# One Trainium2 core, a gated cross-attention layer with eight experts: weight pieces two to a slot, a router in column groups, contexts scored by VectorE

## The reference

```python
def xattn(ctx, adj, W, b):                    # adj is the layer-normed x
    si = einsum('bnd,d->bn', ctx, W[0, :256]); sj = einsum('bnd,d->bn', ctx, W[0, 256:])
    return 0.6 * sigmoid(si[:, :, None] + sj[:, None, :] + b[0]) + 0.4 * adj

def ffn(x, wg, W, b):                         # 4096 tokens of 1024, 8 experts
    logits = x @ wg; probs = softmax(logits); idx = argmax(probs); gate = probs[idx]
    return gate * (x @ W[idx].T + b[idx])     # top-1 routing

x = x + tanh(g_xattn) * xattn(ctx, layernorm(x), ...)
x = x + tanh(g_ffn) * ffn(layernorm(x), ...)
```

## Time and profile before

| what | us |
|---|---|
| median of three timed runs | 689.08 |
| lowest and highest of them | 683.34, 689.30 |
| profiled execution, span | 687.3 |
| TensorE busy | 576.6 (84%) |
| VectorE busy | 445.2 (65%) |
| GpSimd busy | 331.8 (48%) |
| ScalarE busy | 274.1 (40%) |

### The profile page before, as it was taken

How to read it: one execution, slowest core, us unless ns; L and a number is a source line. 1 busy time by engine, 2 the same in 40 slices (tenths; PEclk the granted TensorE clock), 3 DMA queues, 4 the chain that set the end, 5 groups by cost and what they waited for, 6 DMA issues and landing times.

```text
span 687.3 us, 14019 instructions
## 1 busy us (share of the span) xinstructions
PE 576.6 (84%) x2841; PEld 461.2 (67%) x2842; DVE 445.2 (65%) x557; ACT 274.1 (40%) x408; POOL 331.8 (48%) x489
## 2 busy tenths in 40 slices
PE   7898889888707969979779997995999799699990
PEld 5576667666505848858567885884888588588870
DVE  3357778697699885856784587588378557843420
ACT  2367766686424333413333333333343233333220
POOL 1446777788623336325336533633633364356540
PEclk8569999999957989989989998997999899899995
DMA  7911577576679876764776497577756656545530
GB/s 262 403 40 33 175 261 237 198 217 223 239 258 259 238 214 190 225 208 152 224 220 196 147 243 213 189 219 215 217 168 204 189 166 198 164 132 186 182 126 13
DMA packets 83666, 134.72 MB, mean 196 GB/s; under 512 B 11568, under 2 KB 64304, under 8 KB 83504
## 3 DMA queue, kind: packets, MB, share of 16 engines
q1 hardware_dynamic: 73712, 99.47, 49.4%
q0 software_dynamic: 9792, 33.82, 12.8%
HBM read 99.44 MB, written 35.91 MB: 197 GB/s over the span
## 4 chain that ended last, share of the span: by engine, by line
PE 27%; DVE 23%; issue 19%; ACT 9%; POOL 7%; DMA 6%; DVEq 3%; POOLq 2%; ACTq 2%; SPq 1%
PE pair L1058 12%; DVE wt L782 7%; PE pair L985 4%; DVE xr L718 4%; ACT wt L598 4%; DVE pair L777 4%; PE pair L996 3%; PE pair L969 3%; PE pair L974 3%; ACT rb L617 2%; DVE rows L804 2%; DMA out_x<-rows,scatter_row 2%; DMA rows<-table 1%; DVE xc_tr L725 1%; POOL out_x L500 1%
## 5 line engine op out<-in xcount | busy, mean ns | idle before, releaser
L1058 PE MATMUL pair<-wt,xt 128*128 x1728 | 416.2, 404 | 62.6 <-DVE rows L804 41.6
L1058 PEld LDWEIGHTS pair<-wt,xt 128*128 128x128 f32 x1728 | 336.9, 196 | 141.5 <-issue 66.5
L488 POOL TENSOR_TENSOR rows<-rows,rb 128x1024 f32<-128x1024 f32 x37 | 88.7, 2398 | 164.2 <-ACT rb L617 162.6
L782 DVE TENSOR_TENSOR wt<-pair,wt 128x1024 f32 (+1 forms) x64 | 77.5, 1212 | 32.7 <-ACT wt L598 32.7
L598 ACT ACTIVATE wt<-pair 128x1024 f32 (+1 forms) x64 | 64.2, 1024 | 77.7 <-DVE pair L777 70.1
L604 ACT ACTIVATE xt<-pair 128x1024 fp32r<-128x1024 f32 x38 | 39.0, 1026 | 133.0 <-DVE pair L790 110.6
L777 DVE STREAM_TRANSPOSE pair<-w_raw 128x1024 f32<-128x1024 f32 x64 | 79.7, 1250 | 1.9
L790 DVE STREAM_TRANSPOSE pair<-xb 128x1024 f32<-128x1024 f32 x38 | 47.7, 1255 | 46.5 <-issue 26.3
L804 DVE SCALAR_TENSOR_TENSOR rows<-pair,scal,rows 128x1024 f32<-128x1024 f32 x36 | 46.0, 1278 | 44.6 <-PE pair L1058 44.2
L617 ACT ACTIVATE rb<-bias_bc,scal 128x1024 f32 (+1 forms) x37 | 46.0, 1244 | 48.4 <-POOL scal L485 41.1
L794 DVE TENSOR_TENSOR xt<-pair,xt 128x1024 fp32r<-128x1024 f32 x38 | 46.4, 1221 | 28.1 <-ACT xt L604 25.9
(11 more groups left out here) (123 smaller groups left out, 417.9 us busy)
## 6 DMA issues: line engine op xcount, KB each, us to landing
w_raw<-in_L_ffn_W SPq DMA_DIRECT2D x256, 128.0 KB
xb<-table SPq DMA_DIRECT2D x156, 128.0 KB
rows<-table SPq DMA_DIRECT2D x38, 520.0 KB
xr<-in_x SPq DMA_DIRECT2D x32, 512.0 KB, 6.9
ctx_in<-in_ctx SPq DMA_DIRECT2D x8, 512.0 KB, 4.9
bias_bc<-in_L_ffn_b SPq DMA_DIRECT2D x8, 512.0 KB
out_x<-rows,scatter_row POOLq DMA_INDIRECT x36, 4.2
table<-xr,pos POOLq DMA_INDIRECT x32, 4.5
```

The source lines that it names most:

```text
L488: nc.gpsimd.tensor_tensor(rows[:, k, 0:H], rows[:, k, 0:H], rb[:, :], ALU.add).then_inc(base_ready, 1)
L782: nc.vector.tensor_tensor(where[:, :, 1].rearrange("p a k o -> p (a k) o"), ps[:, :].rearrange("p (k o) -> p k o", k=K), where[:, :, 0].re ...
L1058: last = nc.tensor.matmul(out_ps[r % 2][:, HALF * h:HALF * (h + 1)], xt[:, r % RING, x_part, k, :], wt[:, bass.ds(par, 1), w_part, k, HALF ...
```

## The change

- **Weight pieces.** Every expert now gets at least four slots (LEAST = 4), and each of the first four slots of an expert turns two pieces of the next expert's weights (STEP = 2). `w_raw` holds two pieces instead of four; the pair for the next slot is asked for when both pieces of this one are turned, in four transfers of 256 KB. The bias comes in quarters.
- **Slots.** The rows are turned one slot ahead instead of two, `xt` has two buffers instead of three, `rows` four instead of three. The loops have turns of 4 written-out slots (TensorE 2). The first 32 slots (SURE) run without a test; 28 more may be used, so the loops go to 60 instead of 42.
- **Squares.** ACT squares the rows in the slot (`square` on `rows`) and not in the tile stage; POOL waits for it.
- **Router.** The router's weights are padded to 32 columns, and the eight blocks go to four column groups of the array (`tile_position=(0, j)`), two in each; the copy of the logits has 128 rows and a folding matrix `fold` adds the four groups.
- **Transposed tiles.** They have one PSUM buffer (pair 0) instead of two; ACT copies both halves, DVE none.
- **Contexts.** Groups 0 and 1 are scored by DVE straight from the loaded rows (16 instructions of 128x256 with a running sum, two diagonal matrices of 128x512) and spread by one matmul each. Groups 2 to 7 are turned behind tiles 0, 2, 5, 7, 13 and 15.
- **First weights.** The first expert's pieces are turned behind tiles 9, 11, ... 23, and cut behind the next tile. SP asks for them between the loads of x tiles; from the third on, the load waits until the piece two before is turned, and x tiles queue behind it.
- The small loads of the start go through ACT's queue.

```diff
+    LEAST = 4
+    STEP = K // LEAST
+    RING = 4
+    TURN = 4
+    SURE = E * LEAST
+    SLOTS = SURE + N // P - LEAST
+        CTX_TURN = {0: 2, 2: 3, 5: 4, 7: 5, 13: 6, 15: 7}
+        PIECE = {9 + 2 * m: m for m in range(K)}
 @sync
+            def load_first_piece(m):
+                if m >= STEP:
+                    sp.wait_ge(w0_turned, m - STEP + 1)
...
             for t in range(RX, T):
+                if t % 2 and t // 2 - 6 < K:
+                    load_first_piece(t // 2 - 6)
                 sp.wait_ge(row_stored[slot_of(t)], 16)
...
+            def slot(t, r, i):
+                kind = sp.value_load(slot_tab[0:1, 0, bass.ds(t, 1)], min_val=0, max_val=2)
+                rows2, rows3 = row_of(t + 2), row_of(t + 3)
+                if not (isinstance(t, int) and t < 2):
+                    settled(out_stored[(r + 2) % RING], 16 * i + 16 * (r // 2))
+                load_rows(sp, rows2, r + 2)
+                with sp.If(kind > 1):
...
+                    settled(w_turned, STEP * g + STEP)
+                    load_pieces(row0)
+                settled(xb_turned, t + 2)
+                load_blocks(sp, rows3, r + 3)
 @gpsimd
+                settled(sq_ready, u + 1)
+                nc.gpsimd.tensor_scalar(scal[:, k, 0:1], scal[:, k, 8:9], 1.0 / H, EPS, ...)
 @scalar
+            def slot(t, r, i):
+                k = (r + 1) % RING
+                square(t + 1, k, i + (r + 1) // RING)
+                xt_high(t + 1, (r + 1) % 2, cut_a)
+                exp_sum(t + 1, k)
+                with act.If(kind > 1):
+                    for m, ps in enumerate((cut_b, cut_a)):
+                        settled(w_turned, STEP * g + m + 1)
...
+                scaled_bias(t + 1, k, e1, act.snap(e1 % 2))
 @vector
+            def score(t, place_, w0, scale):
+                return nc.vector.scalar_tensor_tensor(out=junk[t], in0=ctx_in[...], scalar=scale,
+                    in1=w_flat[:, w0:w0 + D], op0=ALU.mult, op1=ALU.mult, accum_out=place_)
...
+                if t in PIECE:
+                    first_turn(PIECE[t])
+                if t - 1 in PIECE:
+                    first_low(PIECE[t - 1])
...
+            def slot(t, r, i):
+                settled(xt_ready, t + 1)
+                turn_rows(t + 1, k, TURN // 2 * i + (r + 1) // 2)
+                with dve.If(kind > 1):
...
+                    settled(w_ready, STEP * g + K)
+                    settled(w_landed, 64 * g + 64)
+                    turn_piece(0, cut_b)
+                    xt_low(t + 1, k)
+                    settled(xt_ready, t + 2)
+                    turn_piece(1, cut_a)
+                    cut_low(0, cut_b)
+                    cut_low(1, cut_a)
+                    settled(w_ready, STEP * g + K + STEP)
+                with dve.Else():
+                    xt_low(t + 1, k)
+                settled(base_ready, t + 1)
+                nc.vector.tensor_scalar(scatter_row[...], rows[..., TOK:TOK + 1].bitcast(I32), beyond[:, bass.ds(t, 1)], None, ALU.max)
+                settled(summed, t + 1)
+                nc.vector.scalar_tensor_tensor(...).then_inc(finished, 1)
+            with dve.Fori(0, SURE // TURN) as i:
+                for r in range(TURN):
+                    slot(TURN * i + r, r, i)
+            with dve.Fori(SURE // TURN, SLOTS // TURN) as i:
+                for r in range(TURN):
+                    with dve.If(work > 0):
+                        slot(TURN * i + r, r, i)
 @tensor
+                pe.wait_ge(xc_copied[1], t + 1)
                 for k in range(K):
+                    j = COLS * (k % 4)
+                    last = nc.tensor.matmul(lgt_ps[j:j + COLS, r, :], wg_sb[:, k, :], xc_tr[:, t % 2, k, :],
+                                            start=(k < 4), stop=(k >= K - 4), tile_position=(0, j))
```

More of the change, by code:

```diff
@@ L275, in _ @@
         def _(sp):
-            for g in range(2):
-                sp.dma_start(ctx_in[:, g, :], group_of(ctx_t, g)).then_inc(ctx_landed[g], 16)
-            with nc.allow_non_contiguous_dma(reason="512 weights, once, as columns"):
-                sp.dma_start(wcol[:, :], mix_w.rearrange("a (c p) -> p (a c)", p=P)).then_inc(wcol_landed, 16)
-            sp.dma_start(gates[:, 0:1], g_xattn.unsqueeze(0).to_broadcast([P, 1])).then_inc(gates_landed, 16)
-            sp.dma_start(gates[:, 1:2], g_ffn.unsqueeze(0).to_broadcast([P, 1])).then_inc(gates_landed, 16)
@@ L669, in _ @@
+            with act.Fori(0, SURE // TURN) as i:
+                for r in range(TURN):
+                    slot(TURN * i + r, r, i)
+            with act.Fori(SURE // TURN, SLOTS // TURN) as i:
+                for r in range(TURN):
+                    work = act.value_load(slot_tab[0:1, 0, bass.ds(TURN * i + r, 1)], min_val=0, max_val=2)
+                    with act.If(work > 0):
+                        slot(TURN * i + r, r, i)
                     with act.Else():
@@ L798, in finish @@
-            def finish(t, r):
-                settled(base_ready, t + 1)
-                s = r % RING
-                nc.vector.tensor_tensor(scatter_row[:, s:s + 1], rows[:, s, TOK:TOK + 1].bitcast(I32),
-                                        beyond[:, bass.ds(t, 1)], ALU.max)
-                settled(summed, t + 2)
-                nc.vector.scalar_tensor_tensor(out=rows[:, s, 0:H], in0=out_ps[r % 2][:, :], scalar=scal[:, s, 7:8],
-                                               in1=rows[:, s, 0:H], op0=ALU.mult, op1=ALU.add).then_inc(finished, 1)
@@ new lines, in _ @@
+            link(nc.vector.tensor_tensor(e_f[:, :], e_f[:, :], nth[:, :], ALU.add))
+            link(nc.vector.scalar_tensor_tensor(out=early[:, :], in0=nth[:, :], scalar=float(LEAST), in1=not_last[:, :],
+                                                op0=ALU.is_lt, op1=ALU.mult))
+            nc.vector.tensor_copy(slot_tab[:, 3, :], e_f[:, :])
+            nc.vector.tensor_scalar(e_f[:, :], e_f[:, :], float(STEP * P), float(H + STEP * P), ALU.mult, ALU.add)
+            nc.vector.tensor_tensor(slot_tab[:, 0, :], early[:, :], used[:, :], ALU.add)
@@ new lines, in _, with turn_rows @@
+            with nc.allow_low_precision("whole numbers"):
+                nc.vector.reduce_sum(in_place[:, :], used[:, 0:SLOTS].rearrange("p (a s) -> p s a", s=RING), AX.X)
+            dve.drain()
+            nc.vector.tensor_scalar(slot_tab[:, 4, :], e_f[:, :], float(E * H - STEP * P), None,
+                                    ALU.min).then_inc(slots_told, 1)
+            def turn_rows(u, k, n):
+                settled(xb_landed[k], 64 * n + 64)
+                nc.vector.transpose(turned(cut_a), blocked(xb[:, k, :, :])).then_inc(xb_turned, 1)
@@ L950, in _, with spread @@
                 nc.tensor.matmul(pair[1][:, 0:P], ones, ones, start=True, stop=True)
-            pe.wait_ge(masks_ready, 1)
+            def spread(g):
+                pe.wait_ge(diag_ready, g + 1)
+                nc.tensor.matmul(sj_sum(g), ones, xc_tr[:, g, 0:GR, :], start=True, stop=True).then_inc(sj_summed, 1)
             def turn_context(g):
                 pe.wait_ge(ctx_landed[g % 2], 16 * (g // 2 + 1))
-                if g > 1:
-                    pe.wait_ge(sj_ready, 1 if g == 2 else g)
-                    pe.wait_ge(si_ready, 1 if g == 2 else g)
+                pe.wait_ge(sj_ready, g)
+                if g > 2:
+                    pe.wait_ge(si_ready, g - 2)
                 for c in range(GR):
@@ L1004, in logits_by_token @@
                 for r in range(GR):
-                    last = nc.tensor.matmul(lg_ps[:, r, :], lgt[:, r, :], ident[0:E, 0:E], start=True, stop=True)
+                    last = nc.tensor.matmul(lg_ps[:, r, :], lgt[:, r, :], fold[:, :], start=True, stop=True)
                 last.then_inc(by_token, 1)
```

596 lines of the change are left out of this document (262 added, 334 removed).

## The result

The changed kernel takes 656.55 us (median of four runs, 655.68 to 658.61), the kernel before 686.52 in the four runs beside them (683.34 to 689.30): ratio 0.9567, interval 0.9525 to 0.9609. The time lies in the predicted range, 20.6 us above the forecast of 636. The profiled execution took 657.35, its span is 655.7 us; 31.6 less than before.

A forecast was written before the change was run, and what follows sets the result against it. The slot stage was taken as bound by TensorE, with holes made by VectorE. The terms gave 687.3 - 48.5 + 14 - 10 - 5 - 3 = 634.8, so 636 us as timed median, range 608 to 676.

The forecast's parts named there:

- Start, -10: Up to tile 1's add: tile 0 3.5 us earlier, tile 1 4.4 us after it, together -10 us.
- Slots, -48.5: Slot stage: VectorE's slot with pieces takes 12.2 us, stage falls to 409.3 us, -48.5 (bounds -61.5 and -39).
- the lag: Slots: VectorE may lag TensorE by 6.2 us, gains 1.25 per slot with pieces, regains 6.2 in a fifth; 13 us stops.
- rival 3: Slots: each slot waits for its own weights, a round of 14.3 us instead of 12.2, time 696; 5%.
- Tail, +14: After the last slot: 24 skipped slots instead of 6, at 1.1 us each, 26.4 against 12.1 us: +14.
- the prediction's own sign: Slots and tail: prediction wrong if VectorE's lag does not stop at 6.2, or skipped slots cost over 2 us each.
- The bound of +36: Tail: upper bound, 24 skipped slots at VectorE's old pace of 2.02 us each.
- Tile stage, -5: Tile 1 to tile 31: 14 tiles at 4.2 us and those with pieces at 4.7, sum 134, -5 us.
- rival (2): Tile stage: column groups run one after another, or x tiles come late; it gains nothing or loses +11: 646; 12%.
- TensorE at 1.2 GHz costed at nothing: Tile stage: at 1.2 GHz transposes of 2.2 us and router of at most 2 still fit the 4.2 a tile.
- The rule on mode changes: Tile stage: changing tiling mode drains TensorE, twice each tile; by it the router's gain could vanish.
- Between the stages, -3: Last store to the slots' start: cuts and a piece leave the chain, -3 us (bounds 0 and -5).

The follow-up runs named there:

- run 4: Changed kernel with the scatter row made by `tensor_tensor` on 32-bit integers as before, in place of `tensor_scalar`: 680.60 us (one run).
- runs 1 to 3: Changed kernel with: only 36 slots (614.05 us); SyncE alone testing once per turn of four (638.22); second loops' end read from the table (613.67).
- Run 5: Changed kernel with the first weights' loads two x tiles later in SyncE's order: 648.71 us (one run).
- Run 7: Changed kernel with 24 matmuls, their result overwritten, ahead of each tile's transposes to keep TensorE busy: 655.53 us (one run).
- run 8: Changed kernel with both the first weights' loads two x tiles later and 24 overwritten matmuls ahead of each tile's transposes: 650.05 us (one run).
- runs 6 and 12: Changed kernel with the router in one group of 8 rows: 664.74 us; the same plus first weights' loads two x tiles later: 655.90 us.
- run 9: Kernel before the change with only the scatter row made by `tensor_scalar`, `beyond` in f32: 678.93 us (median of ten), ratio 0.9827 to before.
- run 10: Changed kernel with second loops ending at the last filled turn and first weights loaded two x tiles later: 607.85 us, ratio 0.8866 to before.

## Why the prediction was right or wrong

**Direction and range** held, because the largest term did: TensorE stopped for VectorE, whose slots took up to 17.7 us, and with slots of 11.3 it no longer does. That the sum is off by no more than 20.6 us is in part luck: the slots gave 11.4 us more than forecast, against 34.4 us lost in the tile stage and the tail. Of the forecast's own sum:

- **Start, -10 against -9.8.** Right in the sum, by two misses that cancel: tile 0's add came 1.7 us earlier (28.70 to 27.04) where I had 3.5, and tile 1's 2.7 us behind it where I had 4.4. (The scores took 0.42 us each, the 0.4 that I took.)
- **Slots, -48.5 against -59.9: inside the bounds and mis-sized, by two errors that partly cancel.** First, I took the slot to be 12.2 us, with the scatter row's wait behind GpSimd in ten of fourteen; the changed operation does not wait at all. With it put back, run 4 has 12.34, so that the 12.2 was right for the kernel I had in mind, and I read over the one word of the diff, `tensor_scalar`, that made it another. Second, the lag. I let a piece-free slot give back 6.2 us and counted 13 us of stops; at 12.34 my count would give 15, and run 4 has 21.8. After a piece-free slot VectorE took 16.41 us for the next (355.92 to 372.33), because it waited 2.17 and 4.03 us for ScalarE, whose copies stand behind the bias and the sum of exponentials, and these had waited 2.18 and 3.43 us for GpSimd. In the changed kernel the slot in that place takes 15.36, but it lags so little otherwise that it does no harm.
- **Weights from one buffer** (rival 3): VectorE waited 2.4 us in all for `w_raw` in the slots. The cover was there.
- **Tail, +14 against +36.2: the step that failed.** I listed VectorE, ScalarE and GpSimd and left out SyncE, though the trace of before has its table loads (L332, six from 670.4 to 682.5, 2.4 us apart, the slowest of all). Its queue takes 2.28 us for a skipped slot and sets the end (runs 1 to 3). By the prediction's own sign, skipped slots that cost more than 2 us each, this part was wrong. The bound of +36 that I gave for VectorE was reached by another engine. And what follows the last slot on GpSimd, 3 to 4 us of closing and 6.1 to the end, was in none of my terms.
- **Tile stage, -5 against +7.2: wrong.** I had named the new wait on SyncE, the turning at tile t - 8, and priced it at 0.5 us a tile (4.7 against 4.2). It makes 5.2 while pieces come. Run 5 takes it out and the stage is 136.0, near the 134 of the sum, though not by its terms: VectorE waits 22.5 us for TensorE there, of which the sum had nothing. Late x tiles are the second half of rival (2), at 7.2 us of its 11. What I missed is that by the code the wait closes a circle: the piece's turning waits in VectorE's order behind statistics for an x tile, which waits on SyncE behind the load that waits for the piece before. A wait in such a circle doesn't cost its length once, it sets the pace.
- **TensorE at 1.2 GHz costed at nothing**: not shown. The clock did fall, to 0.70 in the mean. Run 7 raised it and the stage was as long, but as the balance of 5.5 us lost and 5.6 won; with the x tiles on time (run 8 against run 5) what it gave from tile 10 on was 1.9 us, not clear of the spread.
- **The rule on mode changes** (the Trainium skill, "TensorEngine Tiling (Array Packing)", section "Key Properties") made it possible that the router gains nothing; runs 6 and 12 show a gain of 5.6 and 7.7 us in the stage, and no time lost at a change.
- **Between the stages, -3 against -5.3**: right in direction, 0.3 beyond its bound of -5.

What stays open: how the slots' gain divides between the spread pieces and the shorter loops. Why a skipped slot costs SyncE 2.28 us and the other engines 0.85 to 1.2. It fits a fetch of code, since fewer visited places made it cheaper, but no record names it. And run 9's slots: the wait went over into other waits in the execution that was profiled, but not what lengthened the gaps without a releaser from 25.8 to 35.7 us.

## What to carry to other kernels

When a change multiplies empty trips of a loop, read the table loads of every queue in the trace, SyncE's too, and multiply the slowest; better, read the loop's end from the data, which was worth 43 us here. When a load is put ahead of others on an in-order queue, follow its wait back until it ends outside the loop; if it comes back to a load behind it, it sets the pace, and moving it two tiles down was worth 9.8 us in the stage. When added work raises a clock and the time stays, cut the stage in parts before calling the clock free: here 5.5 us lost and 5.6 won stood behind the equal times.

## What the runs showed of the hardware that was not expected

- A VectorE `tensor_tensor` on a single column (0.15 us alone) does not end before GpSimd's add over 128x1024 in SBUF does: ends at 277.23 and 277.21 in run 4. The same holds in run 10 for one with 32 columns of floats and a GpSimd `tensor_scalar` (163.93 and 163.89). `tensor_scalar` of VectorE on the same column takes 0.21 us in the midst of such an add.
- A skipped slot costs 2.28 us on SyncE, against 0.85 on ScalarE, 0.88 on GpSimd, 1.02 on VectorE and 1.2 on TensorE's queue; a skipped turn of four behind one test costs SyncE 1.30.
- A loop whose end is read from the data costs nothing clear over one with a fixed end (spans 613.6 and 612.3, within what runs of the same kernel differ by).
- Sixteen router matmuls of four column groups took 0.64 us at full clock and 1.08 at half, right behind the transposes.
